# A selective scan on Trainium2: two rows of channels in one scan instruction, and the tensor engine's inputs made in pairs

## What is computed

```python
delta = softplus(einsum('er,brl->bel', dt_proj_w, dt_lo) + dt_proj_b[None, :, None])
A = -exp(A_log)
def step(state, xs):                       # over l = 0..511
    d_t, B_t, C_t, u_t = xs
    dA = exp(d_t[..., None] * A)
    state = state * dA + (d_t * u_t)[..., None] * B_t[:, None, :]
    y_t = einsum('ben,bn->be', state, C_t)
    return (state, y_t)
y = y + D[None, :, None] * u
y = y * silu(z)
...
x = x + xattn(ctx, layernorm(x), ...)
x = x + ffn(layernorm(x), w_gate, w_up, w_down, ln_weight)
```

## Time and profile before

| | before |
|---|---|
| median of 3 runs | 586.08 us (585.56 to 587.4) |
| the profiled execution | 586.31 us, span 584.4 us |
| DVE, scans (line 897) | 256, 286.7 us busy |
| POOL, products (line 470) | 63, 286.4 us busy |
| PE, additions (line 1221) | 1024 matmuls, 156.0 us busy |
| PE, inputs (lines 1205 and 1208) | 768 and 640 matmuls, 102.3 and 97.8 us busy |
| ACT, factors (line 682) | 256, 165.5 us busy |
| granted PE clock, mean | 0.991 |

### The profile page before, as it was taken

The page is one execution under the profiler, slowest core; times in us unless marked ns, Lnnn a source line. Parts: engine busy times, 40 slices in busy tenths (PEclk is TensorE's granted clock), DMA queues, the critical chain, the costliest instruction groups (busy, mean ns, idle before and its releaser), DMA issues.

```text
span 584.4 us, 10287 instructions
## 1 busy us (share of the span) xinstructions
PE 541.3 (93%) x3667; PEld 404.7 (69%) x3684; DVE 540.5 (92%) x820; ACT 512.1 (88%) x755; POOL 464.5 (79%) x184
## 2 busy tenths in 40 slices
PE   5898987999999999999999888998889999999996
PEld 2335476899998989989999888995334444444442
DVE  3999979999999999999999999997998999999873
ACT  1899999999999999989999799998967868778673
POOL 4888374999999899999999999994564765666662
PEclk9999999999999999999999899899999999999998
DMA  9992690221112741127331194234532533424321
GB/s 285 407 364 73 230 309 11 56 65 64 55 55 91 163 117 65 59 63 202 88 98 55 55 228 168 62 128 106 104 65 63 109 81 78 112 65 97 94 54 55
DMA packets 62194, 68.65 MB, mean 117 GB/s; under 512 B 41136, under 2 KB 41136, under 8 KB 59968
## 3 DMA queue, kind: packets, MB, share of 16 engines
q1 hardware_dynamic: 59776, 63.59, 36.3%
q0 software_dynamic: 2368, 4.40, 4.5%
HBM read 50.02 MB, written 8.52 MB: 100 GB/s over the span
## 4 chain that ended last, share of the span: by engine, by line
DVE 28%; PE 26%; ACT 17%; POOL 12%; issue 11%; DMA 5%; SPq 0%; DVEq 0%; POOLq 0%; ACTq 0%
POOL arena L470 11%; ACT arena L682 8%; PE ps L1221 8%; PE ps L1205 6%; ACT arena L607 5%; DVE arena L808 5%; PE ps L1208 4%; PE ps L1263 4%; PE ps L1256 3%; DVE arena L897 3%; DVE arena L985 3%; DMA arena<-arena 2%; DVE bst_x L840 2%; DVE am L954 1%; DMA arena<-x 1%
## 5 line engine op out<-in xcount | busy, mean ns | idle before, releaser
L470 POOL TENSOR_TENSOR arena<-arena 128x2048 f32<-128x2048 f32 x63 | 286.4, 4592 | 13.2 <-DVE arena L897 11.1
L897 DVE TENSOR_TENSOR_SCAN arena<-arena,ps 128x512 f32<-128x512 f32 x256 | 286.7, 1197 | 2.0 <-ACT arena L682 0.5
L682 ACT ACTIVATE arena<-arena,a_neg 128x512 f32<-128x512 f32 x256 | 165.5, 712 | 9.5 <-DVE arena L897 9.2
L1221 PE MATMUL ps<-ident,arena 128*128 128x128 f32 x1024 | 156.0, 276 | 6.7 <-POOL arena L470 3.4
L1221 PEld LDWEIGHTS ps<-ident,arena 128*128 128x128 f32 x1024 | 121.2, 142 | 10.7 <-POOL arena L470 6.2
L504 POOL TENSOR_TENSOR arena<-arena 128x1024 f32<-128x1024 f32 x30 | 71.1, 2371 | 57.2 <-DVE arena L985 57.2
L1256 PE MATMUL ps<-arena 128*128 128x512 bf16 x504 | 112.9, 379 | 2.1 <-DVE arena L985 1.1
L1205 PE MATMUL ps<-arena 128*128 128x128 f32 x768 | 102.3, 276 | 3.4 <-ACT arena L607 2.1
L1208 PE MATMUL ps<-ident,arena 128*128 128x128 f32 x640 | 97.8, 277 | 5.2 <-DVE arena L897 2.9
L607 ACT ACTIVATE arena<-arena,bT 128x512 f32<-128x512 f32 x160 | 102.0, 711 | 0.0
L1205 PEld LDWEIGHTS ps<-arena 128*128 128x128 f32 x768 | 93.3, 192 | 5.2 <-ACT arena L607 2.3
(11 more groups left out here) (121 smaller groups left out, 578.1 us busy)
## 6 DMA issues: line engine op xcount, KB each, us to landing
arena<-w_all SPq DMA_DIRECT2D x16, 1024.0 KB, 9.2
arena<-c_rows SPq DMA_DIRECT2D x64, 256.0 KB, 3.2
arena<-x SPq DMA_DIRECT2D x4, 1024.0 KB, 15.8
w_ternary<-arena SPq DMA_DIRECT2D x8, 512.0 KB, 4.2
arena<-w_ternary SPq DMA_DIRECT2D x8, 512.0 KB, 5.0
arena<-x POOLq DMA_DIRECT2D x4, 1024.0 KB, 10.0
out<-arena SPq DMA_DIRECT2D x16, 256.0 KB, 2.0
arena<-ctx_t SPq DMA_DIRECT2D x4, 512.0 KB, 13.7
```

Of the source, the lines that this page charges most:

```text
L470: nc.gpsimd.tensor_tensor(hs[:, k % RING, :, :], hs[:, k % RING, :, :], c_bc[:, s:s + 1, :].to_broadcast([P, KE, L]), ALU.mult).then_inc(S ...
L682: nc.scalar.activation(dA[:, s, i, :], delta_u[:, b, 0, i, :], ACT.Exp, scale=a_neg[:, i, n:n + 1]).then_inc(S["dA_ready"], 1)
L897: nc.vector.tensor_tensor_scan(out=hs[:, k % RING, i, :], data0=dA[:, k % 2, i, :], data1=ps[:, 4 + i, :], initial=0.0, op0=ALU.mult, op1= ...
L1221: last = mm(ps[:, c, i * P:(i + 1) * P], hs[:, k % RING, i, c * P:(c + 1) * P], ident[:], start=(n == 0 and i == 0), stop=(n == DS - 1), i ...
```

## The change

One scan instruction now covers two rows, h = 0 (rows 0 and 1) and h = 1 (rows 2 and 3), 1024 elements that lie one behind the other in `dA`, in two neighbouring banks of PSUM and in `hs`. For the state not to run on from one row into the next, the decay factor at the first position of rows 1 and 3 is zero: four memsets write it once, in both halves of `dA`, and ACT's Exp of these rows now leaves that first column out (511 elements). A step counts two in `scan_done` in place of four, and all waits for it are restated so. PE makes both inputs of a pair, and then does both additions of the pair.

```diff
@@ gpsimd, product(k) @@
-                pool.wait_ge(S["scan_done"], k * KE + KE)
+                pool.wait_ge(S["scan_done"], k * 2 + 2)
@@ scalar @@
                     for i in range(KE):
-                        hold(act, "scan_done", (k - 2) * KE + i + 1)
-                        nc.scalar.activation(dA[:, s, i, :], delta_u[:, b, 0, i, :], ACT.Exp,
+                        hold(act, "scan_done", (k - 2) * 2 + i // 2 + 1)
+                        nc.scalar.activation(dA[:, s, i, i % 2:], delta_u[:, b, 0, i, i % 2:], ACT.Exp,
                                              scale=a_neg[:, i, n:n + 1]).then_inc(S["dA_ready"], 1)
@@ vector @@
             keep_duT(3, 1)
+            for i in range(2):
+                for j in (1, 3):
+                    own.done(nc.vector.memset(dA[:, i, j, 0:1], 0.0))
+            own.wait()
...
             def scan(k):
-                for i in range(KE):
+                for h in range(2):
                     if k >= RING:
-                        hold(dve, *added(k - RING, i // 2))
-                    dve.wait_ge(S["dA_ready"], k * KE + i + 1)
-                    dve.wait_ge(S["dBu_ready"], k * KE + i + 1)
-                    nc.vector.tensor_tensor_scan(out=hs[:, k % RING, i, :], data0=dA[:, k % 2, i, :],
-                                                 data1=ps[:, 4 + i, :], initial=0.0, op0=ALU.mult,
+                        hold(dve, *added(k - RING, h))
+                    dve.wait_ge(S["dA_ready"], k * KE + 2 * h + 2)
+                    dve.wait_ge(S["dBu_ready"], k * KE + 2 * h + 2)
+                    rows = slice(2 * h, 2 * h + 2)
+                    nc.vector.tensor_tensor_scan(out=flat(hs[:, k % RING, rows, :]), data0=flat(dA[:, k % 2, rows, :]),
+                                                 data1=flat(ps[:, 4 + 2 * h:6 + 2 * h, :]), initial=0.0, op0=ALU.mult,
                                                  op1=ALU.add).then_inc(S["scan_done"], 1)
-                    if k >= DS and k % DS == 2 and i == 1:
+                    if k >= DS and k % DS == 2 and h == 0:
                         gate_y(k // DS - 1)
...
-            dve.wait_ge(S["scan_done"], LAST * KE + KE)
+            dve.wait_ge(S["scan_done"], LAST * 2 + 2)
@@ tensor, turn(k, i) @@
-                hold(pe, "scan_done", (k - 1) * KE + i + 1)
+                hold(pe, "scan_done", (k - 1) * 2 + i // 2 + 1)
@@ tensor, the loop @@
             for k in range(NB * DS):
-                for i in range(KE):
+                for h in range(2):
                     if k + 2 <= LAST:
-                        turn(k + 2, i)
+                        turn(k + 2, 2 * h)
+                        turn(k + 2, 2 * h + 1)
                     if k > 0:
-                        add(k - 1, i)
-                        if 4 <= (k - 1) % DS < 4 + KL:
-                            add_skip((k - 1) // DS, i, (k - 1) % DS - 4)
+                        for i in (2 * h, 2 * h + 1):
+                            add(k - 1, i)
+                            if 4 <= (k - 1) % DS < 4 + KL:
+                                add_skip((k - 1) // DS, i, (k - 1) % DS - 4)
...
-            pe.wait_ge(S["scan_done"], NB * DS * KE)
+            pe.wait_ge(S["scan_done"], NB * DS * 2)
```

## The result

| | before | after |
|---|---|---|
| median (5 runs each) | 586.08 us | 597.43 us (596.21 to 598.92) |
| ratio of after to before | 1 | 1.0192 (1.0174 to 1.0210) |
| the profiled execution | 586.31 us, span 584.4 | 598.92 us, span 597.0 |
| POOL, idle before products | 13.2 us | 24.8 us |
| DVE, idle before scans | 2.0 us | 16.6 us |

Slower by 11.3 us. The direction was forecast. The forecast of 5.6 us was half of what was measured, and the range ended 0.4 us under the median. Timed twice more beside other kernels, the changed kernel came to 598.34 and 598.95, with ratios of 1.0228 (1.0206 to 1.0250) and 1.0220 (1.0200 to 1.0241).

A forecast was written before the change was run, and what follows sets the result against it. Four engines were within 2% in the scan stage, POOL slowest at 4.52 us a step. DVE's -5.7 + 14.3 - 2.8 + 0.6 = +6.4, less 0.3 and 0.5, gave +5.6: 591.7 us, range 587.3 to 597.0.

The forecast's parts named there:

- scans of 1024: DVE's scans: a pair in one instruction takes 2.178 us instead of 2.222, saving 5.7 us of DVE in all.
- DVE's waits of before: DVE in the scan stage: 2.8 us of waits, put down to POOL's lag through PE's queue, would go.
- stalls at diagonal steps at full clock: DVE waiting for PE's inputs at diagonal steps: 0.61 us each, 1.03 at step 11, together 14.3 us over 64 steps.
- stalls behind falls of the clock: PE at 1.2 GHz: nothing in the sum; only a rival gave it +1 us for each fall.
- memsets: Four one-column memsets and a wait ahead of the first scan, without cover: 0.6 us (0.2 to 1.0).
- first scan, from ahead of the stage: Start of the first scan: forecast at 93.9 us, with no delay counted beyond the 0.6 us for memsets.
- The handover: DVE and PE at diagonal steps: inputs 0.14 us late, plus 0.47 from additions before the second inputs; 0.61 together.
- the first part: First pair of a diagonal step: PE needs 2.23 us where DVE leaves 2.09, so 0.14 late.
- rival 1: The scan saves nothing, or PE's clock falls more often (+1 us each): 595 to 599 us, chance 0.13.
- The end of the stage: POOL's last product: 0.3 us of its 0.44 lag goes, step 63's stall takes 0.5 off; +6.4 becomes +5.6.
- Rival 2: No change or faster, POOL stays the bound if a diagonal step stalls under 0.43: 583.7 to 586.6 us, chance 0.12.
- The rule: Breaking instructions up helps where an unsaturated vector engine causes bubbles elsewhere; cited as speaking against the change, no size given.

The follow-up runs named there:

- the profile without a fall: Shown with the changed kernel whose PE idle stretches were filled by repeated inputs: 311.7 us from first scan's start to last one's end, 16.5 us of stalls.
- PE's order alone: Kernel before, scans of one row, with only PE's loop changed to both inputs of a pair, then both additions: 584.46 us, ratio 0.9986; again 584.05, 0.9981.
- PE light: Changed kernel with diagonal steps' inputs made by transposes, 4 matmuls a row in place of 8, scaling by B left out: 584.32 us, ratio 0.9983.

## Why the prediction was half right

From the first scan's start (95.23) to the last one's end (408.74 + 2.29 = 411.03) are 315.8 us in the profile of the changed kernel: 278.9 of scans (127 x 2.178 + 2.29), 7.1 of gates and 9.2 of breaks as before, and 20.6 left for stalls. Against before, DVE ended 14.2 later; forecast were 6.4. Of the stalls 4.1 stand behind the three falls of the clock (1.2, 1.2 and 1.7 over the ordinary ones at steps 1, 20 and 54), which leaves 16.5, as in the profile without a fall.

| term of the sum | forecast | measured in this profile |
|---|---|---|
| scans of 1024 | -5.7 | -5.7 |
| DVE's waits of before | -2.8 | -2.8 |
| stalls at diagonal steps at full clock | +14.3 | +16.5 |
| stalls behind falls of the clock | 0 | +4.1 |
| memsets | +0.6 | +0.2 |
| first scan, from ahead of the stage | 0 | +1.7 |
| sum | +6.4 | +14.0 (14.2 by the ends) |

- *The saving per scan* was right: 2.178.
- *The handover* was right in its place, its two parts and its sign: 0.47 was forecast for the additions between and 0.48 measured. The size of the first part was off: 0.21 for 0.14. I took 1.94 for the inputs of a pair and got 2.02, because PE's first matmul after a wait takes longer (0.185 us to the next one for 0.111; before has it too: 1.13 for a row of 8 behind a wait, 1.06 otherwise). Another 0.03 goes when DVE starts again. 0.72 for 0.61, 2.2 us in all, is the second term that was mis-sized.
- *The step that failed* is the term of PE's clock, which the sum puts at nothing. I had the falls in rival 1, at 1 us each and as something that replaces the forecast: they come on top of it. The reason, that a mean of 0.991 in before means few falls, did not carry over, since the prediction itself makes PE wait more. In the stage there were 3 (twice) and 5, for 2 in before, and they came where DVE had nothing to spare. In the three profiles they cost 4.1, 4.1 and 6.1 us of stall, and side by side the kernel without them was 4.1 us faster. Without falls the changed kernel is at 594.5 to 594.8 us, inside the range; with them its three medians are above it. In the five executions first timed, whose median has a clock of 0.991, the falls come to some 2.7 us by the slope above, an estimate; the handover's 2.2 is most of the rest.
- *Rival 1*, at 595 to 599, holds the result, by one of its two conditions. The scan does save its 0.044; that the range held is the clock's doing alone.
- *DVE's waits of before* were put down to POOL's lag. They are gone as forecast (step 27 now stalls as step 11 does, 0.58 and 0.48); the row repeats the forecast, since all waits after stand in the two rows below it. That POOL's lag was their source is not shown: PE's order alone already takes the 1.04 us at step 27 away.
- *Memsets*: 1.35 from the last copy's start to the first scan, 1.13 before. 0.2 for the assumed 0.6.
- *The first scan's other 1.7* are this execution's own: with the memsets in it, the first scan came 1.9 later than before in this profile, 0.8 in the second and 0.1 in the third. The change doesn't touch what runs there. This execution was the slowest of the five, 1.5 above their median.
- *The end of the stage*: the last product started at 406.60 for 392.82, 13.8 later: DVE's 14.2 less the stall of step 63, as forecast, but with POOL's lag at 0.65 for 0.44. The 0.3 that I had counted as lost with the lag were still there, and 0.2 more. So the product that was to end at 403 ended at 411.15, and POOL's idle time grew by 11.6 us for the 5 forecast. The spans differ by 12.6, so 1.2 came back behind the stage. In before the clock fell at 571 inside the feed-forward stage, in after it didn't; that this is the 1.2 was not tested.
- *Rival 2* named the right floor: with half of the matmuls of the diagonal inputs taken out, POOL's pace sets the time, and the gain of the wide scan does not reach it. What it put at 583.7 to 586.6 came to 584.32. For the changed kernel itself it was wrong, since a diagonal step stalls by 0.72 and not under 0.43.
- *The rule* that breaking instructions up may let work finish sooner (the Trainium skill, Perfetto Trace Analysis, Optimizing Scalar/DVE Operations) is stated for an engine that isn't saturated but causes bubbles on others. Here DVE was as good as saturated, so the rule did not apply as it stands, but what happened goes its way: 11 us lost for a wider scan that saves 5.7 on DVE. The 125 ns or so for each DVE instruction on PSUM of the same section do not fit this case: merging two scans saves 44 (2.222 to 2.178).

## What to carry to other kernels

Merging two instructions saves one fixed part (44 ns here) and doubles the grain at which buffers change hands; so compare, for each buffer, the time that the other engine has between release and need with what it must do in it, latencies included, before counting the saving. If the merge is still wanted, give the partner an order that fits the new grain, with no more other work between two handovers than its wait lasts (here one addition in place of two took 7 us off). And where several engines are balanced within a few per cent, ask first which one is the floor, since a gain on another is worth only the floor's idle time.

## What was not expected of the hardware

- PE's granted clock fell to 1.2 GHz for 3.4 us behind waits of PE (1.4 to 3.5 us between two matmuls) in all three profiles of the changed kernel. Not each such wait draws a fall: PE waits 1.79 us at each of the three gates, and the first gate drew one in two profiles, the second and third in the other; a wait of 2.81 us at 380 us drew none twice. Which waits draw a fall is left open.
- Repeated matmuls in those waits made the kernel 4.1 us faster (594.82 for 598.95), and the changed kernel's own executions take longer by some 0.85 us for each fall that their mean clock shows.
- The same fall costs 0 to 0.5 us (PE's order alone, PE light) or 0.6 to 1.7 (the changed kernel), by what is to spare at the handover behind it.
